# The opening of a two-layer cross-attention kernel: loads in another order, projections in halves, and the first cross keys made one block later

## The reference

```python
# x: (16, 56, 128), ctx: (16, 1500, 96), all float32
# layer 0, 16 heads of 8
q, k, v = split(x @ w_qkv + b_qkv)
x = layer_norm(x + mha(q, k, v) @ w_so + b_so)
qc = x @ w_q + b_q;  kc = ctx @ w_k + b_k;  vc = ctx @ w_v + b_v
x = layer_norm(x + mha(qc, kc, vc) @ w_co + b_co)
x = layer_norm(x + relu(relu(x @ w1 + b1) @ w2 + b2) @ w3 + b3)
# layer 1: another cross attention over the same ctx, 16 heads of 64, added to x
```

## Time and profile before

| | |
|---|---|
| runs | 1092.0, 1093.75, 1091.74 us |
| the profiled execution's own time | 1092.7 us |
| its span in the trace | 1090.9 us |
| mean granted TensorE clock | 0.963 |
| opening, first instruction to the next block's first | 0.25 to 23.15 us |
| self attention | 23.15 to 59.8 us |
| PE, DVE, ACT, POOL busy over the span | 93, 68, 52, 35% |

### The profile page before, as it was taken

One profiled execution on the slowest core, in us unless ns is written; L12 is line 12 of the kernel. 1 busy time (PEld: TensorE's weight loads), 2 busy tenths in 40 slices (PEclk: granted clock), 3 DMA queues, 4 the chain that ended last, 5 costly groups with the idle time before them and its releaser, 6 DMA issues. The chain is left out here.

```text
span 1090.9 us, 31627 instructions
## 1 busy us (share of the span) xinstructions
PE 1011.2 (93%) x12044; PEld 738.5 (68%) x12044; DVE 742.7 (68%) x1406; ACT 566.7 (52%) x1135; POOL 377.8 (35%) x273
## 2 busy tenths in 40 slices
PE   5956999999999999889679999999999999999997
PEld 2642677777777777646327777777777777777786
DVE  4846888778887787311796676767677676767752
ACT  2632777677776776631444444444445444445442
POOL 4612111121111213020106554445555454555542
PEclk8976999999999999979799999999999999999998
DMA  3504444543445432120021211111011111111100
GB/s 117 129 13 132 130 136 143 146 135 121 133 141 149 136 101 87 31 71 0 1 60 41 57 57 58 43 50 41 35 57 55 55 39 53 39 37 57 35 4 4
DMA packets 47022, 79.90 MB, mean 73 GB/s; under 512 B 6979, under 2 KB 33813, under 8 KB 46965
## 3 DMA queue, kind: packets, MB, share of 16 engines
q1 hardware_dynamic: 46964, 79.11, 24.5%
HBM read 50.93 MB, written 21.96 MB: 67 GB/s over the span
## 5 line engine op out<-in xcount | busy, mean ns | idle before, releaser
L1374 ACT ACTIVATE P<-PS 125x448 f32<-125x448 f32 x384 | 207.1, 544 | 265.1 <-PE PS L1283 263.2
L1264 POOL TENSOR_TENSOR Pl<-P 125x896 f16<-125x896 f32 x128 | 229.9, 1801 | 237.0 <-ACT P L1374 237.0
L1010 DVE TENSOR_REDUCE m<-PS 128x1 f32<-128x500 f32 x336 | 220.6, 674 | 114.9 <-PE PS L1001 113.0
L916 DVE TENSOR_REDUCE m_part<-PS 128x1 f32<-128x500 f32 x336 | 210.3, 672 | 60.5 <-PE PS L818 58.9
L1299 PE MATMUL PS<-cNh,P 125*128 125x97 f16 x1344 | 198.0, 208 | 0.1
L1301 PE MATMUL PS<-cNh,Pl 125*128 125x97 f16 x1344 | 197.4, 207 | 0.0
L1300 PE MATMUL PS<-cNl,P 125*128 125x96 f16 x1344 | 196.8, 206 | 0.0
L894 ACT ACTIVATE Pb<-PS 125x448 f32<-125x448 f32 x384 | 186.0, 547 | 19.7 <-PE PS L793 18.7
L1300 PEld LDWEIGHTS PS<-cNl,P 125*128 125x128 bf16 x1344 | 131.9, 98 | 25.4
L818 PE MATMUL PS<-KH,Qmx 128*128 128x500 f16 x336 | 129.4, 387 | 14.2 <-PEq L690 8.2
L1299 PEld LDWEIGHTS PS<-cNh,P 125*128 125x128 bf16 x1344 | 131.1, 98 | 15.7 <-issue 3.2
(11 more groups left out here) (167 smaller groups left out, 1489.0 us busy)
## 6 DMA issues: line engine op xcount, KB each, us to landing
Kst<-k_halves SPq DMA_DIRECT2D x144, 125.0 KB, 2.8
k_halves<-KH SPq DMA_DIRECT2D x16, 750.0 KB, 3.3
cx<-in_ctx SPq DMA_DIRECT2D x16, 562.5 KB
d_cx<-in_ctx SPq DMA_DIRECT2D x16, 562.5 KB
c_halves<-cHi SPq DMA_DIRECT2D x16, 281.2 KB, 2.7
c_halves<-cLo SPq DMA_DIRECT2D x16, 281.2 KB, 3.1
cTh<-c_halves SPq DMA_DIRECT2D x16, 281.2 KB, 3.1
cTl<-c_halves SPq DMA_DIRECT2D x16, 281.2 KB, 4.0
```

Of the source, the lines that this page charges most:

```text
L916: nc.vector.tensor_reduce(m_part[:, t, part:part + 1], PS[:, 6 + k % 2, 0:SP], AX.X, ALU.max).then_inc(s_reduced, 1)
L1010: nc.vector.tensor_reduce(m21[:, t, part:part + 1], PS[:, S1[k % 2], 0:SP], AX.X, ALU.max).then_inc(n_red, 1)
L1264: nc.gpsimd.tensor_tensor(Pl[:, c % NP], P1[:, c % NP], high, ALU.subtract).then_inc(n_low_p, 1)
L1374: nc.scalar.activation(P1[:, c % NP, half * HALF:(half + 1) * HALF], PS[0:KC, u % 3, 0:HALF], ACT.Exp).then_inc(n_exp, 1)
```

## The change

`wqkv` and `bqk` are loaded ahead of the first context and get semaphores of their own. X is copied in halves, so that the products on the first half don't wait for the second. PE makes, for the first 448 tokens, keys and then queries, then turns all three context pieces, then does keys and queries for the second 448 tokens. DVE adds the bias in four instructions of half the size; POOL begins on its own keys after the first. ACT rounds `wkv` ahead of the context. The cross keys of the first batch leave the opening: PE makes them in step 0 of the self attention behind the scores, ACT keeps them ahead of the exponential of step 0, DVE splits them after the subtraction of step 0, and PE waits at the head of step 1 (behind its scores) for all three splits, since their banks (now 4, 5, 6) are used next.

```diff
-                return {T_BANK: (4, 5, 6), K_BANK: (7, 4, 5)}[banks][k]
+                return 4 + k
@@ SP, opening
+                sp.dma_start(wqkv[:], w_qkv).then_inc(qkv_in, 16)
+                sp.dma_start(bqk[:], ...).then_inc(bqk_in, 16)
                 load_context(sp, -1, 0, 2)
-                sp.dma_start(wqkv[:], w_qkv).then_inc(qkv_in, 16)
-                sp.dma_start(bqk[:], ...).then_inc(qkv_in, 16)
@@ POOL, opening
-                pool.wait_ge(qk_kept, 2)
+                pool.wait_ge(qk_kept, 1)
@@ PE, opening
-                mm.then_inc(x_turned, 1)
-                turn_context(pe, -1, 0, 0, mode=OPEN)
-                pe.wait_ge(qkv_in, 32)
-                pe.wait_ge(x_kept, 1)
-                for s in range(2):
-                    for half in range(2):
-                        mm = pe.matmul(...)
-                    mm.then_inc(qk_made, 1)
-                    turn_context(pe, -1, 0, s + 1, mode=OPEN)
-                pe.wait_ge(wkv_split, 1)
-                pe.wait_ge(ct_ones, 1)
-                for k in range(NSP):
-                    k_piece(pe, -1, 0, k, mode=OPEN)
+                    if t % 4 == 3:
+                        mm.then_inc(x_turned, 1)
+                pe.wait_ge(qkv_in, 16)
+                for half in range(2):
+                    pe.wait_ge(x_kept, half + 1)
+                    for s in (1, 0):
+                        pe.matmul(...).then_inc(qk_made, 1)
+                    if half == 0:
+                        for k in range(NSP):
+                            turn_context(pe, -1, 0, k, mode=OPEN)
@@ DVE, opening
+                dve.wait_ge(bqk_in, 16)
+                for half in range(2):
+                    for at, (s, rows_of) in enumerate(((1, SKT), (0, SQT))):
+                        dve.wait_ge(qk_made, 2 * half + at + 1)
+                        nc.vector.tensor_scalar(<448 columns of rows_of>, PS[:, 2 * s + half, 0:HALF], bqk..., ALU.add).then_inc(qk_kept, 1)
+                    if half == 0:
+                        for k in range(NSP):
+                            split_context(dve, -1, 0, k, mode=OPEN)
                 dve.wait_ge(wkv_high, 1)
                 nc.vector.scalar_tensor_tensor(out=wkv16[:, :, 1, :], ...).then_inc(wkv_split, 1)
-                for k in range(NSP):
-                    split_keys(dve, -1, 0, k, mode=OPEN)
@@ ACT, opening
+                act.wait_ge(wkv_in, 64)
+                nc.scalar.activation(wkv16[:, :, 0, :], wkv[:], ...).then_inc(wkv_high, 1)
                 for k in range(NSP):
                     keep_context(act, -1, 0, k, mode=OPEN)
-                for k in range(NSP):
-                    keep_keys(act, -1, 0, k, mode=OPEN)
@@ ACT, self attention, ahead of the exponential
+                    if isinstance(t, int) and t == 0:
+                        for k in range(NSP):
+                            keep_keys(act, -1, 0, k, mode=OPEN)
@@ PE, self attention, behind the scores
+                    if isinstance(t, int) and t == 0:
+                        first_keys()          # waits wkv_split, ct_ones; three k_pieces
+                    if isinstance(t, int) and t == 1:
+                        pe.wait_ge(k_split, NSP)
@@ DVE, self attention, behind the subtraction
+                    if isinstance(t, int) and t == 0:
+                        for k in range(NSP):
+                            split_keys(dve, -1, 0, k, mode=OPEN)
```

More of the change, by code:

```diff
@@ L355, in lay_own_keys @@
                                     spread(tab[:, C_M8:C_END], 2, SQ), ALU.mult).then_inc(s_kbd, 1)
-        table_in, x_in, qkv_in, bv_in, wkv_in, later_in = (
-            sem("table_in"), sem("x_in"), sem("qkv_in"), sem("bv_in"), sem("wkv_in"), sem("later_in"))
+        table_in, x_in, qkv_in, bqk_in, bv_in, wkv_in, later_in = (
+            sem("table_in"), sem("x_in"), sem("qkv_in"), sem("bqk_in"), sem("bv_in"), sem("wkv_in"), sem("later_in"))
         wkv_high, wkv_split = sem("wkv_high"), sem("wkv_split")
@@ L367, in _ @@
                 sp.dma_start(X[:], x.rearrange("b q d -> (b q) d").rearrange("(t p) d -> p t d", p=TP)).then_inc(x_in, 16)
+                sp.dma_start(wqkv[:], w_qkv).then_inc(qkv_in, 16)
+                sp.dma_start(bqk[:], b_qkv[0:2 * D].rearrange("(s p) -> p s", p=D), allow_slow_non_contiguous=True).then_inc(bqk_in, 16)
                 load_context(sp, -1, 0, 2)
-                sp.dma_start(wqkv[:], w_qkv).then_inc(qkv_in, 16)
-                sp.dma_start(bqk[:], b_qkv[0:2 * D].rearrange("(s p) -> p s", p=D), allow_slow_non_contiguous=True).then_inc(qkv_in, 16)
                 for which, (weight, bias) in enumerate(((w_k, b_k), (w_v, b_v))):
@@ L394, in _ @@
                     mm = pe.transpose(PS[:, t // 4, (t % 4) * TP:(t % 4 + 1) * TP], X[:, t, :], ident[0:TP, 0:TP])
-                mm.then_inc(x_turned, 1)
-                turn_context(pe, -1, 0, 0, mode=OPEN)
-                pe.wait_ge(qkv_in, 32)
-                pe.wait_ge(x_kept, 1)
-                for s in range(2):
-                    for half in range(2):
-                        mm = pe.matmul(PS[:, 2 * s + half, 0:HALF], wqkv[:, s * D:(s + 1) * D],
-                                       T128[:, half * HALF:(half + 1) * HALF], start=True, stop=True)
-                    mm.then_inc(qk_made, 1)
-                    turn_context(pe, -1, 0, s + 1, mode=OPEN)
-                pe.wait_ge(wkv_split, 1)
-                pe.wait_ge(ct_ones, 1)
-                for k in range(NSP):
-                    k_piece(pe, -1, 0, k, mode=OPEN)
+                    if t % 4 == 3:
[4 more added lines that the diff above has]
+                    for s in (1, 0):
+                        pe.matmul(PS[:, 2 * s + half, 0:HALF], wqkv[:, s * D:(s + 1) * D],
+                                  T128[:, half * HALF:(half + 1) * HALF], start=True, stop=True).then_inc(qk_made, 1)
+                    if half == 0:
+                        for k in range(NSP):
+                            turn_context(pe, -1, 0, k, mode=OPEN)
             @block.vector
@@ L415, in _ @@
                 nc.vector.memset(an[:], 0.0).then_inc(zeros_set, 1)
-                dve.wait_ge(x_turned, 1)
-                nc.vector.tensor_copy(T128[:].rearrange("p (h c) -> p h c", h=2), PS[:, 0:2, 0:HALF]).then_inc(x_kept, 1)
+                for half in range(2):
+                    dve.wait_ge(x_turned, half + 1)
+                    nc.vector.tensor_copy(T128[:, half * HALF:(half + 1) * HALF], PS[:, half, 0:HALF]).then_inc(x_kept, 1)
                 for slot in range(2):
@@ L420, in _ @@
                         nc.vector.tensor_copy(Vbd[:, slot, j, :, 16:18], spread(tab[0:TP, C_MV:C_M8], 1, PAIRS)).then_inc(s_ones, 1)
[L421 to L428, removed]
+                dve.wait_ge(bqk_in, 16)
+                for half in range(2):
+                    for at, (s, rows_of) in enumerate(((1, SKT), (0, SQT))):
+                        dve.wait_ge(qk_made, 2 * half + at + 1)
+                        nc.vector.tensor_scalar(rows_of[:, half * (B // 2):(half + 1) * (B // 2)].rearrange("p b q -> p (b q)"), PS[:, 2 * s + half, 0:HALF],
+                                                bqk[:, s:s + 1], None, ALU.add).then_inc(qk_kept, 1)
+                    if half == 0:
+                        for k in range(NSP):
+                            split_context(dve, -1, 0, k, mode=OPEN)
                 dve.wait_ge(wkv_high, 1)
@@ L431, in _ @@
                                                op0=ALU.mult, op1=ALU.subtract).then_inc(wkv_split, 1)
-                for k in range(NSP):
-                    split_keys(dve, -1, 0, k, mode=OPEN)
             @block.scalar
             def _(act):
+                act.wait_ge(wkv_in, 64)
+                nc.scalar.activation(wkv16[:, :, 0, :], wkv[:], ACT.Identity, scale=WS).then_inc(wkv_high, 1)
                 for k in range(NSP):
                     keep_context(act, -1, 0, k, mode=OPEN)
-                    if k == 0:
-                        act.wait_ge(wkv_in, 64)
-                        nc.scalar.activation(wkv16[:, :, 0, :], wkv[:], ACT.Identity, scale=WS).then_inc(wkv_high, 1)
-                for k in range(NSP):
-                    keep_keys(act, -1, 0, k, mode=OPEN)
         LATER = 19
@@ L541, in own_values, with first_keys @@
                     mm.then_inc(s_v, 1)
+                def first_keys():
+                    pe.wait_ge(wkv_split, 1)
+                    pe.wait_ge(ct_ones, 1)
+                    for k in range(NSP):
+                        k_piece(pe, -1, 0, k, mode=OPEN)
                 def step(t, slot):
```

## The result

The changed kernel takes 1086.2 us (median of 4 runs, 1085.35 to 1086.5), beside 1092.88 for the kernel before in the same measurement. The ratio is 0.9932 [0.9918, 0.9946]: 6.7 us less by the medians, 7.4 by the ratio, where 4.4 was forecast. By its ratio the kernel stands at 1084.6 on the scale of the 1092.0 above, under the forecast range. Two later measurements of the same kernel give 0.9953 [0.9938, 0.9968] and 0.9956 [0.9942, 0.9970]. Over all sixteen runs the median is 1087.1, against 1093.0 for the 68 runs of the kernel before (all measurements together, on several chips): 5.9 us. So the sign and the order of the gain were right, its size was forecast too small, and the first measurement was at the lucky end.

What follows compares the result with a forecast made beforehand. The prediction took the opening's chain through several engines as the bound, since blocks follow each other. Opening -5.7 and self attention +1.3 gave -4.4, from 1092.0 to 1087.6 us; range 1085.7 to 1091.7.

Steps and rivals of the forecast that it cites:

- the term for the opening: Opening: removed key stretch (3.6) and PE's earlier start (2.1) start the self attention at 17.4 instead of 23.15, 5.7 us gained.
- the term for the self attention: Self attention, step 0: the moved cross keys lose 1.3 us, bounds -1.4 to +3.6.
- behind the self attention: Later blocks: all earlier by about 4.4, nothing further gained; another clock level here and there can differ by 1.4.
- `Kbd` off the path: Opening, POOL: `Kbd` of the first step needs only the first quarter, so it doesn't set the end.
- One sign of being wrong: Opening: ACT waiting for `wkv` while turned context stands in PSUM would show the prediction wrong.
- DVE's three splits, 2.12, from 5.9 to 8.0: Self attention, step 0: the term that counts, making PE's transposes 1.2 late, at 8.06 instead of 6.87.
- The other path of the forecast: Self attention, DVE: value bias, maximum and subtraction of step 1 behind the splits end at about 10.75.
- second rival: Self attention: PE's clock is high through step 0, gain 5.9, time 1086.1; chance 0.10.
- first rival: Self attention: PE's clock is low through step 0, loss 3.6 instead of 1.3, time 1089.9; chance 0.15.
- The third rival: Opening: the context lands late behind `bqk`, at 15.6; 1.9 us slower, time 1093.9; chance 0.09.
- The fourth: Self attention's end or later projections: the opening's gain returns as a wait or low clock, time 1091.6; chance 0.10.
- what was forecast to take the last place: Self attention's end: SP's wait for later weights, released at 49.3, replaces POOL's L504 (about 49.2) at about no cost.

Runs made afterwards that it cites:

- adding one wait to the kernel before: The kernel before, with POOL laying its first own keys only when the rest of `wkv` is made: 0.9990, 1091.98 us.
- the keys moved alone: The kernel before with only the first cross keys moved into step 0 of the self attention; loads, X and projections as before: 0.9984, 1090.95 us.
- The kernel with the other order, above: The changed kernel with ACT rounding `wkv` behind the first context cast, as before the change: 0.9958, 1088.95 us.
- the first repetition: The changed kernel unchanged, measured a second time with six runs: 0.9953 against the kernel before.
- the context loaded first: The changed kernel with the first context loaded ahead of `wqkv` and `bqk` again, their own semaphores kept: 0.9972, 1090.19 us.
- the first piece at the start: The changed kernel with the first of three cross key pieces made, cast and split early in the self attention block: 0.9939, 1086.62 us.
- the first trace: The profile of the changed kernel from its first measurement: 1086.2 us, ratio 0.9932 against the kernel before.
- the second repetition: The changed kernel unchanged, measured a third time: 0.9956 against the kernel before.
- POOL behind the second half: The changed kernel with POOL's first own keys held until the keys of both halves have their bias: 0.9965, 1088.86 us.
- a second set: The changed kernel with DVE's three cross key splits done twice in step 0, PE and SP waiting for the second: 0.9975, 1089.67 us.

## Why the prediction missed: the right chain, with mis-sized terms

The forecast gain was 4.4 and the first measurement gave 7.4 by its ratio. The 3.0 between them are 0.7 in the term for the opening, 0.8 in the term for the self attention, 0.9 behind the self attention, and 0.6 between the pair of traces (6.8) and the ratio. The first two are errors of the forecast, the other two did not come again in full.

**The opening, forecast 5.7, measured 6.4.** The chain was the forecast one: L401 at 7.97 (8.2 forecast), `wqkv` no wait, the context waited for until 11.47 (11.33), PE's end at 14.5 (15.25), DVE's rest of `wkv` last, start at 16.74 (17.4). Two sizes in it were off, and one of them made the difference. The rest of `wkv` was priced at the 0.92 of its row, although that row stands beside POOL's `Kbd`, and the text itself moves `Kbd` away: 0.41, shown by adding one wait to the kernel before. And the clock had risen by the end of the first products, so all twelve transposes took 1.49 instead of 2.25; that gave nothing, because DVE's queue behind ACT's casts (12.51 to 14.01) ended its second bias half at 16.12, where 16.1 was forecast. I named `Kbd` off the path without seeing that in the kernel before it stood 0.2 ahead of closing the opening itself; the keys moved alone show it (POOL to 20.81). One sign of being wrong did appear, for 0.2 us: ACT waited for `wkv` until 12.18 while the first turned context piece was ready at about 12.0 (an estimate, a third of the 1.49 behind 11.47). The kernel with the other order, above, starts no earlier, so it cost nothing that can be seen.

**The loss in the self attention, forecast 1.3, measured 0.53.** This is the step that failed most: "DVE's three splits, 2.12, from 5.9 to 8.0". They ran from 5.31 to 7.15. The row holds idle time between its instructions; back to back they take 1.84. They began at 5.31 mostly because the values took 0.77 instead of 1.20, the clock being higher. With the splits done at 7.15, the exponential was the last to end, at 7.28; it had been forecast at 7.4, and ahead of the splits. It stands behind ACT's casts and ends 0.47 later than the 6.81 of before. (The other path of the forecast, DVE's subtraction of step 1, ended at 9.61; its forecast 10.75 is also 0.2 more than its own rows give from 8.0 on.) So the transposes came at 7.42 (8.06 forecast, 6.87 before), and these 0.55 are the loss, to 0.02. Which of the two ends last differs between executions. In the traces with the high clock in step 0's scores and key products (the first repetition, the context loaded first, the first piece at the start) the transposes wait for the splits, 0.75 to 0.81. In those with several key products at the low clock (the first trace, the second repetition, the keys moved alone, POOL behind the second half) they wait for the exponential, 0.25 to 0.26. The term forecast as the only one that counts was one of two that end within 0.6 us of each other; that more splits than these delay everything is shown (1.76 for a second set). With the clock high through step 0 the first reciprocal is 8.95 after the start (second rival, which had 9.28), with the clock low 12.66 (first rival, 13.1). Both rivals were real, as executions and not as kernels.

**Behind the self attention, forecast 0 with 1.4 either way, measured 0.9.** 5.9 us of advance leave the self attention, 6.8 arrive. The first norm takes 0.4 less, and there are such pieces later. I can show that this stretch varies with the clock between two traces of one kernel (9.61 and 11.24); that it gave 0.9 in the first measurement was luck: between the first reciprocal and the end the traces of the repetitions lose 1.7 and gain 0.6. The medians of all runs, -5.9, are what the opening and step 0 explain, and the forecast's own error is 1.5.

**The third rival, the context late behind `bqk`'s 256 elements.** It didn't occur. The context was waited for until 11.47, 0.93 later than before, of which its issue (2.74 instead of 1.66) explains all. The 9.0 us of `bqk` were time behind the context in the queue and not its own: issued ahead of the context, it landed 4.4 us after its issue, and 8.5 after it when the context was put first again. The prediction took from the rule that it cites for such a load that `bqk` delays the context; with 256 elements no delay beyond the later issue shows.

**The fourth, the end not moving with the start.** Not seen. SP's wait for the later weights grew from 4.8 to 6.1, while L498 began 6.0 earlier than its like before, with no wait in front. SP was released at 46.8 (its last issue ended at 40.7), where 49.3 was forecast; 1.5 of that is the splits, done at 23.89 and not at 25.4. That is only 0.8 ahead of L498 at 47.63: what was forecast to take the last place just missed it.

Open: how the clock's stretches are placed in an execution. No kernel here controls them, and the runs of one kernel, which order mostly by their mean clock, lie further apart (5.7 us) than most parts of this change are worth.

## What to carry to other kernels

When a chain is shortened, ask for each instruction left on it whether its duration and its place belong to it or to a neighbour: the last 0.5 us came from a POOL instruction that no longer ran beside DVE's, and one part of the change alone gave only 1.4, in part because that same instruction became the end. Moving work across a block's border pays if it lands where its engine waits for another, and costs where one in-order queue has the next step's work right behind it; split such work, and put the first piece into the gap at the start. A merged row such as "x3 2.12" is an envelope, not a price.

## What the runs showed of the hardware

- A DVE instruction on 97x256 elements (f32 in, f16 in and out) takes 0.41 alone and 0.86 to 0.92 beside a running POOL instruction on 128x448; that one takes 1.83 for two alone and 2.02 to 2.07 beside it.
- A load issued behind one on 125 partitions landed about when that one does: `wqkv` at 10.94, where the context, in the kernels that load it first, was waited for until 10.12 to 10.54. Issued ahead, `wqkv` caused no wait at 7.97.
- 256 single numbers (`bqk`, 1 KB) landed 4.4 us after their issue with `wqkv` ahead of them, and 8.5 to 9.0 us after it with the 562.5 KB context ahead.
- One kernel on one chip differs by 5.7 us between executions (1084.9 to 1090.7), mostly in the order of their mean clock. Differences below 1 us between kernels can be read in the traces at like clock, but hardly in six runs.
